# Two-layer transformer block on one core: layer 0's stack loads with the copies as the inner dimension

## What is computed

```python
x_norm = modulate(_ln(x), shift_a, scale_a)
q, k, v = jnp.split(x_norm @ W_qkv + b_qkv, 3, axis=-1)      # each to (B, 16, 512, 8)
attn_w = jax.nn.softmax(jnp.einsum('bhqd,bhkd->bhqk', q, k) * scale, axis=-1)
attn_out = jnp.einsum('bhqk,bhkd->bhqd', attn_w, v)
x = x + gate_a[:, None] * (attn_out @ W_proj + b_proj)
# then cross-attention on the context, and x + gate_m * mlp(...)
```

## Time and profile before

| | us |
|---|---|
| median of 3 runs | 507.16 |
| profiled execution | 507.0 |
| its span, first to last instruction | 505.3 |
| PE busy | 383.8 (76%) |
| DVE busy | 303.5 (60%) |
| ACT busy | 204.4 (40%) |
| POOL busy | 109.4 (22%) |
| mean granted TensorE clock | 0.814 of full |

### The profile page before, as it was taken

One profiled execution on the slowest core, in us unless ns is written; L12 is line 12 of the kernel. 1 busy time (PEld: TensorE's weight loads), 2 busy tenths in 40 slices (PEclk: granted clock), 3 DMA queues, 4 the chain that ended last, 5 costly groups with the idle time before them and its releaser, 6 DMA issues.

```text
span 505.3 us, 9017 instructions
## 1 busy us (share of the span) xinstructions
PE 383.8 (76%) x3346; PEld 227.0 (45%) x3346; DVE 303.5 (60%) x1279; ACT 204.4 (40%) x304; POOL 109.4 (22%) x128
## 2 busy tenths in 40 slices
PE   1957990079999899888997969897747657773976
PEld 1744540023223332566765554776335434452554
DVE  4362371059999881556655364323598999998232
ACT  1230000036666568355673313232244545553511
POOL 7044500070000010210012140001044344444010
PEclk9976555559999999989999978556687777877889
DMA  7121311400000000000000000000000000000000
GB/s 213 32 96 79 147 58 79 141 22 2 3 2 2 0 2 1 1 1 2 2 1 0 1 5 3 7 3 3 1 1 3 0 1 2 1 2 0 2 21 22
DMA packets 10667, 12.16 MB, mean 24 GB/s; under 512 B 2234, under 2 KB 8959, under 8 KB 10623
## 3 DMA queue, kind: packets, MB, share of 16 engines
q1 hardware_dynamic: 10325, 11.55, 6.9%
q0 software_dynamic: 256, 0.01, 0.0%
q10 hardware_dynamic: 42, 0.01, 0.0%
HBM read 8.69 MB, written 2.62 MB: 22 GB/s over the span
## 4 chain that ended last, share of the span: by engine, by line
PE 53%; DVE 24%; issue 10%; ACT 7%; DMA 3%; POOL 1%; SPq 1%; ACTq 0%; DVEq 0%
PE psum L1332 7%; PE psum L1392 5%; PE psum L1360 4%; PE psum L1345 4%; DVE left L1158 3%; DVE left L1165 3%; PE psum L1229 3%; PE psum L1491 3%; DVE mx L1103 2%; PE psum L1375 2%; DVE top L1155 2%; PE psum L1403 2%; DVE top L1162 2%; PE psum L1459 2%; PE psum L1415 2%
## 5 line engine op out<-in xcount | busy, mean ns | idle before, releaser
L1103 DVE TENSOR_REDUCE mx<-psum 128x1 f32<-128x512 f32 x128 | 80.3, 681 | 49.1 <-PE psum L1332 49.0
L717 ACT ACTIVATE big<-psum 128x1024 f32<-128x1024 f32 x64 | 62.3, 1022 | 71.4 <-PE psum L1345 71.1
L1345 PE MATMUL psum<-QS,KS 75*128 75x512 bf16 x128 | 39.4, 395 | 27.1 <-issue 26.7
L1332 PE MATMUL psum<-KS,QS 72*128 72x512 bf16 x128 | 52.4, 448 | 6.3 <-DMA KS<-scr_k 3.1
L547 POOL TENSOR_TENSOR rstd<-vareps,minus_half 128x4 f32<-128x4 f32 x12 | 12.2, 1020 | 197.6 <-DVE vareps L887 197.5
L1392 PE MATMUL psum<-kblk,qf 128*128 128x308 f32 x128 | 47.3, 502 | 1.1 <-DVE qf L1036 0.8
L1403 PE MATMUL psum<-ident,pr 128*77 128x128 f32 x256 | 39.5, 305 | 9.9 <-POOL pr L658 9.8
L1403 PEld LDWEIGHTS psum<-ident,pr 128*77 128x77 f32 x256 | 35.3, 170 | 18.0 <-POOL pr L658 13.3
L658 POOL TENSOR_TENSOR pr<-pr,early 128x616 f32<-128x616 f32 x16 | 23.9, 1492 | 56.1 <-ACT early L827 38.9
L1360 PE MATMUL psum<-big,V 128*9 128x512 f32 x256 | 34.3, 609 | 0.5 <-ACT big L717 0.5
L1332 PEld LDWEIGHTS psum<-KS,QS 72*128 72x128 bf16 x128 | 11.6, 103 | 49.7 <-DVE mx L1103 23.5
(11 more groups left out here) (193 smaller groups left out, 695.3 us busy)
## 6 DMA issues: line engine op xcount, KB each, us to landing
QS<-scr_q SPq DMA_DIRECT2D x8, 288.0 KB
KS<-scr_k SPq DMA_DIRECT2D x8, 288.0 KB
scr_q<-qp SPq DMA_DIRECT2D x2, 384.0 KB, 7.8
scr_k<-kp SPq DMA_DIRECT2D x2, 384.0 KB, 6.1
early<-in_L_xcond_w_ada_dram SPq DMA_DIRECT2D x1, 576.0 KB, 7.8
wmlp<-in_L_xcond_W_mlp_dram SPq DMA_DIRECT2D x2, 256.0 KB, 3.6
scr_k<-kp SPq DMA_DIRECT2D x2, 256.0 KB, 7.8
wm<-in_L_xcond_w_m_dram SPq DMA_DIRECT2D x1, 512.0 KB, 12.3
```

Source lines behind the costliest of these rows:

```text
L717: freed(act.activation(pT[:, u % 2, 1024 * half:1024 * (half + 1)], ps, ACT.Exp), "sT", 0, u, half)
L1103: freed(dve.tensor_reduce(mx[:, n % 3, NT * hh + q:NT * hh + q + 1], ps, AX_X, ALU.max), "max", t, q)
L1332: filled(pe.matmul(ps, QS[b][0:ROWS, h, q * P:(q + 1) * P], KS[b][0:ROWS, h, :], start=True, stop=True), "max", j, q)
L1345: last = pe.matmul(ps[:, t * N:(t + 1) * N], KS[b][0:ROWS + 3, h, kt * P:(kt + 1) * P], QS[b][0:ROWS + 3, h, :], start=True, stop=True)
```

## The change

Only the access patterns of the two stack loads change. In the source (a pattern is a list of [step, count], outermost first) the dimension of the three copies stood outside the 24 rows of (part, dimension); now the 24 rows stand outside and the copies inside. So row r of the destination held copy r // 24 of the 24-row block, and now holds copy r % 3 of (part, dimension) r // 3, in QS and KS alike. The destination is written as 72 rows of one run of 2,048 values. The writes to the scratch, the shape of the scratch, and all other instructions are as before; the source of the KS load is on L455 now instead of L456.

```diff
@@ stack_traffic, for g in range(NG) @@
                 rows = scr_q[b][:, g * w:(g + 1) * w]
-                sp.dma_start(QS[b][0:ROWS, G * g:G * (g + 1), :],
-                             bass.AP(rows.tensor, rows.offset, [[0, 3]] + [list(a) for a in rows.ap])
+                sp.dma_start(QS[b][0:ROWS, G * g:G * (g + 1), :].rearrange("r h t -> r (h t)"),
+                             bass.AP(rows.tensor, rows.offset, [[H * N, 3 * D], [0, 3], [1, w]])
                              ).then_inc(s_stack[b][g], 16)
                 rows = scr_k[b].rearrange("p d n -> (p d) n")[0:3 * D, g * w:(g + 1) * w]
-                one = [list(a) for a in rows.ap]
-                sp.dma_start(KS[b][0:ROWS, G * g:G * (g + 1), :],
-                             bass.AP(rows.tensor, rows.offset, [[D * H * N, 3]] + one)).then_inc(s_stack[b][g], 16)
+                sp.dma_start(KS[b][0:ROWS, G * g:G * (g + 1), :].rearrange("r h t -> r (h t)"),
+                             bass.AP(rows.tensor, rows.offset, [[H * N, 3 * D], [D * H * N, 3], [1, w]])
+                             ).then_inc(s_stack[b][g], 16)
```

## The result

| | before | changed |
|---|---|---|
| median of 4 runs, us | 506.87 | 478.53 |
| lowest, highest | 504.2, 510.65 | 474.67, 479.91 |
| profiled execution, us | 507.0 | 479.91 |
| its span, us | 505.3 | 478.2 |

The ratio is 0.942, with a 95% interval of 0.934 to 0.950. The forecast was 476, the range 465 to 486. In the profiled executions the span is 27.1 us shorter, between the medians it is 28.3; the profiled execution of the changed kernel is the slowest of its four.

A forecast was written before the change was run, and what follows sets the result against it. PE was taken as bound by SP's transfer queue, where slow three-engine stack loads held up the row maxima. Gains of 3.14 + 26.70 + 1.3 = 31.1 us took 507.0 to 475.9, rounded to 476; range 465 to 486.

The forecast's parts named there:

- step 1: Batch 0's first loads: the first KS load lands at 38.5, so PE's wait before the first L1332 goes, -3.14 us.
- step 3: Maxima of the first group land at 71.8, before PE reaches L1345 at 73.8; the stall goes entirely, -26.70 us.
- step 5: TensorE's clock: the 2.4 GHz stretch at 40.8 to 44.2, now filled with work, gives -1.3 us, at most 1.5.
- steps 4 and 5: Behind the stall: no hidden engine work delays PE, and the clock's rise may come sooner or later; both taken as 0.
- Step 2: Batch 1's loads: SP reaches its scratch writes at about 39; at 0.88 us a load, all moved by 51.4, perhaps 55.
- the gain barely depends on the number of engines: With six engines batch 1's loads would end at 65.5, still before the maxima are ready at 68.4.
- The rival that the clock holds: PE keeps 2.4 GHz through the gate matmuls, 44.2 to 69.1, saving up to 12.4 us more: 464.8 us; chance 0.12.
- a clock that stays at 0.50 well beyond nine microseconds: Sign of a wrong forecast: 1.2 GHz lasting that long after the first L1345 would give back some of the gain.

The follow-up runs named there:

- batch 0 alone: New order of source dimensions for batch 0's loads only, batch 1's keeping the copies outermost as in the kernel before: 491.35 us, ratio 0.965.
- destination alone: The changed kernel with the two source dimensions put back (copies outermost), the destination still 72 rows of one run: 507.85 us, ratio 1.004.
- cut 23 and 1: The changed kernel with each load cut into two transfers, of 23 and 1 of the 24 outer rows: 620.63 us, ratio 1.218.
- cut 21 and 3: The changed kernel with each load cut into two transfers, of 21 and 3 of the 24 outer rows: 482.02 us, ratio 0.947.
- copies apart: Rows in the order of the kernel before, but each of the three copies its own transfer of 24 rows: 477.95 us, ratio 0.936.
- batch 1 alone: New order of source dimensions for batch 1's loads only, batch 0's as in the kernel before: 492.14 us, ratio 0.966.
- cut 12 and 12: The changed kernel with each load cut into two transfers of 12 of the 24 outer rows: 479.63 us, ratio 0.939.

## Why the prediction was right

The mechanism was right, and the total nearly so. Of the forecast's 31.1 us the traces show 27.1: 3.6 for 3.14 in step 1, 26.7 for 26.70 in step 3, 2.0 for 1.3 in step 5, and 5.2 lost behind the stall where steps 4 and 5 had 0. That the small misses ahead of the stall went the other way, and took 1.2 us off the error, is luck. So is part of the margin: one wrong size, that of a load, cost nothing only because nothing waited on it.

**The queue and its cause.** Right, and shown: three engines (share 0.19), twelve after (0.75), seven and one where the counts leave seven (0.44) and one (0.06). What the prediction's account of the stall leaves open is how the 26.7 us divide between SP's late issue and the slow landing; both come from the loads ahead.

**Step 1 (-3.14).** Right. PE goes from L1529 to L1332 unhindered; of the lead of 3.6 us, 0.2 is an earlier start of the whole (28.61 against 28.85 for the first scratch write).

**Step 2.** SP reached the scratch writes of batch 1 at 39.38 (39 forecast). The size of a load was off: 288 KB at 206 GB/s is 1.4 us, not 0.88, because the engines did not keep their 27.8 GB/s when twelve ran. The scratch of batch 1 was written at 50.1, some 6 us later than my sum has it (44.3), and batch 1's loads moved until about 63 us, not 51 to 55. It cost nothing, because the maxima came only at 66.1, 3 us behind the end of the loads. But the statement that the gain barely depends on the number of engines, down to six, is not borne out: with seven and three engines in place of twelve, same rows and same number of transfers, 6.68 us of stall are left.

**Step 3 (-26.70).** Right: the stall is 0. SP issued the maxima at 66.16; with three issues in 1.84 us and the median landing of 1.7 from the last issue's start they were there by about 69.1, before PE at 71.38. The cover, the time by which the maxima were there before PE asked for them, was near 2 us.

**Step 5, first part (-1.3, "at most 1.5").** Too small, and the bound was worked out wrongly. The fast stretch does not shrink when it is filled: the 3.1 us of it in which PE had waited hold, at double pace, work that takes up to 6.2 us at 1.2 GHz. So beside the wait itself up to 3.1 us could be gained, not 1.5. In the stretch at 2.4 GHz a pair of gate matmuls takes 0.49 us, and 0.79 outside it (changed kernel):

```profile
42.66 0.49 PE L1315 MATMUL psum<-early,silu_c 128*128 128x128 f32 x2
...
49.51 0.79 PE L1317 MATMUL psum<-vecs,ident 47*128 47x128 f32 x2
```

The lead before the stall is 76.95 - 71.38 = 5.6 us, so with the 3.6 of step 1 taken off, 2.0 of it are the clock's. The rival that the clock holds did not come: the changed kernel's clock was at 0.97 in 40.8 to 44.2 and at 0.51 in 44.2 to 66, with PE busy all the time (first and second row below).

**Steps 4 and 5, behind the stall (0).** This is where 31.1 us became 27.1. The prediction named this very sign, a clock that stays at 0.50 well beyond nine microseconds, but set it at 0 in the sum. I took the cold stretch behind the first L1345 as 8.8 us, as before. It was 14.0, as the rows of the changed kernel show: 0.50 in 73 to 80, and 0.73 in 80 to 90, so the rise is near 85.4.

```profile
40.80:44.20 3.40, 3.16 (x16) 1.96 (x14) 2.63 (x6) 0.00 (x0) 3.35 (x5) 0.97 0.98 274
44.20:66.00 21.80, 21.65 (x66) 12.78 (x64) 9.92 (x20) 1.58 (x3) 6.37 (x16) 0.51 0.54 163
...
73.00:80.00 7.00, 7.00 (x22) 1.82 (x21) 4.97 (x10) 3.57 (x4) 6.51 (x14) 0.50 0.06 17
80.00:90.00 10.00, 10.00 (x44) 2.67 (x46) 6.80 (x11) 4.92 (x6) 1.04 (x1) 0.73 0.01 2
```

Five more microseconds at 1.2 GHz cost 2.5 (84.5 us from the first score matmul to the last row-maximum matmul, against 82.0). The traces of all the kernels order themselves by this: from the first score matmul to the last row-maximum matmul it took 82 us where the clock rose 8.4 to 9.3 us after the former (before, batch 0 alone, destination alone, cut 23 and 1), 83.5 where it rose after 9.7 (cut 21 and 3, copies apart), and 84.2 to 84.5 where after 13.4 to 14.1 (changed, batch 1 alone, cut 12 and 12). The maxima through ACT fell out (86.6), with its second wait and second fall. What decides when the clock rises was not tried; the stall alone doesn't, since the copies apart had none and rose after 9.7, while batch 1 alone had one of 7.97 us and rose after 13.4.

The other 2.7 us are lost behind the last L1332, where the instructions are the same. The windows from there to the end, before and changed:

```profile
185.70:505.30 319.60, 248.76 (x2744) 166.68 (x2740) 191.49 (x1029) 141.36 (x229) 69.93 (x53) 0.83 0.01 3
```

```profile
155.90:478.20 322.30, 254.22 (x2744) 169.72 (x2740) 191.75 (x1029) 141.41 (x229) 70.03 (x53) 0.80 0.01 3
```

DVE and ACT are busy for the same time within 0.3 us, PE for 5.5 us more, at a mean clock of 0.80 against 0.83. That it is the clock is argued from these rows; it was not tried by itself. It isn't peculiar to the change: it was 321 to 323 us in six of the eight kernels tried, and 319.7 to 319.9 in the other two. And each of these numbers is from one execution: the four runs of the kernel before lie 6.5 us apart and those of the changed one 5.2, so 2.5 and 2.7 us are no more than what one kernel's own runs differ by. That the changed kernel always gives them back is not shown.

## What to carry to other kernels

Where SP issues transfers at a steady interval of several microseconds and the DMA share stands at a fraction k/16, look at the outermost counts of both sides: here a count of 3 outermost confined each load to three engines, and putting 24 there, which shares the divisor 12 with 72, brought no new cost. Then look at who stands behind them in the queue, and not only at when it is issued, but at when it lands: the price was not the loads' own, for which PE waited 3 us, but that of three transfers of 4 KB behind them, for which it waited 27. Issuing the maxima from ACT, with the loads left slow, brought 4.2% where the change brings 5.8%. And TensorE's clock may add to such a gain or take from it: in the traces here it gave 2.0 us, and took 2.5, and 2.7 more if the argument above holds.

## What the runs showed of the hardware

- The time that SP takes to issue a load did not depend on the number of rows: 0.76 us for 72 rows, 0.75 for 36, 0.71 to 0.72 for 9, all with three dimensions in the source; but 0.36 for 24 rows with two. That the number of dimensions makes the difference is the likely reading; row counts and engines were not varied alone.
- Three engines moved 83.5 GB/s, or 27.8 each, and one 26 (90 to 105 us of the cut 23 and 1); twelve moved 206 to 215 together, 17 to 18 each, and 173, or 14.4 each, when no row was read twice in a transfer (copies apart).
- A transfer of 23 outer rows (69 partitions) ran on one engine, one of 21 (63) on seven: 141 us between the cuts 12 and 12 and 23 and 1, which differ in two numbers.
- Three transfers of 4 KB landed 1.7 us after their issue with nothing ahead of them, up to 14.0 us with slow loads ahead of them in SP's queue, and in 2.3 to 4.5 us when ACT issued them beside such loads.
- Through 22 us of nearly uninterrupted work on PE the granted clock stayed at 1.2 GHz (44.2 to 66 us of the changed kernel, PE busy for 21.65 of 21.8; the fp32 matmuls of 128 columns took 11.2 us, the bf16 ones of 512 columns 8.7).
